# Leaving padded list rows out of gathers and scatters, and starting the second mixture stage inside the last tile of the first

## The reference, cut to what matters

```python
def _L1_ffn_ref(x, P_w, U1, U2, U3, W1, W2, b2):
    # x_flat: 2048 x 256; W1: 12 x 1024 x 256; W2: 12 x 256 x 1024
    x_addr = x_flat @ P_w.T
    dw1 = _route_dense(x_addr @ U1.T, 3, 1.0)   # three of 12 experts per token, softmax of their scores
    dw2 = _route_dense(x_addr @ U2.T, 3, 1.0)
    dw3 = _route_dense(x_addr @ U3.T, 3, 1.0)
    h = sum over e of (x_flat @ W1[e].T * dw1[:, e:e+1])
    h = gelu(h, approximate=False)
    y = sum over e of (h @ W2[e].T * dw2[:, e:e+1])
    return y + dw3 @ b2
x = x + _L1_ffn_ref(_layernorm(x), ...)
```

## Time and profile before

| | before |
|---|---|
| median of three runs | 1073.56 us |
| profiled execution | 1068.93 us |
| its span | 1067.1 us |
| TensorE busy in the span | 1019.5 us (96%) |
| VectorE, ScalarE, GpSimd busy | 618.1, 438.9, 285.0 us |
| first stage on TensorE (L2331) | from 587.8 to 799.2 us |
| second stage on TensorE (L2382) | from 802.8 to 1048.9 us |

### The profile page before, as it was taken

One profiled execution on the slowest core, in us unless ns is written; L12 is line 12 of the kernel. 1 busy time (PEld: TensorE's weight loads), 2 busy tenths in 40 slices (PEclk: granted clock), 3 DMA queues, 4 the chain that ended last, 5 costly groups with the idle time before them and its releaser, 6 DMA issues. The chain is left out here.

```text
span 1067.1 us, 19880 instructions
## 1 busy us (share of the span) xinstructions
PE 1019.5 (96%) x6532; PEld 743.3 (70%) x6532; DVE 618.1 (58%) x1388; ACT 438.9 (41%) x856; POOL 285.0 (27%) x313
## 2 busy tenths in 40 slices
PE   8999999999899999999987999999999999999996
PEld 5888844688899888688875444443347777777784
DVE  6988757776544454565777888676411365323513
ACT  2666644422211223366654355554442233333330
POOL 1221100000011100201102222265623577644441
PEclk9999999999999999999999999999999999999998
DMA  8000050000599100470001544489999999764644
GB/s 238 2 0 0 1 195 0 1 1 1 175 343 351 44 1 0 171 316 1 12 31 33 188 168 173 171 290 380 354 352 410 408 340 344 251 224 147 223 133 173
DMA packets 79950, 177.25 MB, mean 166 GB/s; under 512 B 11581, under 2 KB 32047, under 8 KB 78332
## 3 DMA queue, kind: packets, MB, share of 16 engines
q1 hardware_dynamic: 55250, 102.09, 26.4%
q0 software_dynamic: 20896, 69.75, 19.1%
q10 hardware_dynamic: 3722, 4.33, 1.2%
HBM read 126.06 MB, written 47.97 MB: 163 GB/s over the span
## 5 line engine op out<-in xcount | busy, mean ns | idle before, releaser
L2684 DVE COPY shared<-f_psT 128x256 f32<-128x256 f32 x54 | 22.6, 421 | 145.8 <-PE f_psT L2382 145.8
L2432 ACT ACTIVATE shared<-f_psH 128x512 f32<-128x512 f32 x108 | 64.3, 597 | 103.0 <-PE f_psH L2331 82.5
L2331 PE MATMUL f_psH<-W,ctxT 128*128 (+2 forms) x216 | 99.4, 603 | 4.7 <-ACT f_stage L2453 2.3
L2382 PE MATMUL f_psT<-W,sel 128*64 (+2 forms) x432 | 98.6, 381 | 2.6 <-ACT sel L2461 1.4
L2382 PE MATMUL f_psT<-W,f_xg 128*128 x432 | 97.7, 379 | 0.0
L2331 PE MATMUL f_psH<-W,f_xTk 128*128 (+2 forms) x216 | 97.5, 594 | 0.2 <-ACT shared L2432 0.2
L2382 PEld LDWEIGHTS f_psT<-W,f_xg 128*128 128x128 f32 x432 | 80.1, 190 | 9.8
L2382 PEld LDWEIGHTS f_psT<-W,sel 128*64 128x64 f32 (+2 forms) x432 | 62.0, 148 | 28.5 <-issue 5.9
L2141 POOL DMA_INDIRECT f_xg<-xn_d,f_toks x54 | 53.9, 999 | 102.2 <-PE f_psT L2307 90.0
L2141 POOL DMA_INDIRECT f_temps<-h_d,f_toks x54 | 52.7, 977 | 96.9 <-PE f_psH L2359 77.2
L1581 POOL DMA_DIRECT2D m_eos<-m_eo x32 | 16.8, 525 | 200.5 <-DVE m_eo L1478 199.2
(11 more groups left out here) (357 smaller groups left out, 2188.9 us busy)
## 6 DMA issues: line engine op xcount, KB each, us to landing
p_d<-shared SPq DMA_DIRECT2D x108, 256.0 KB, 2.6
W<-in_f_W1T SPq DMA_DIRECT2D x12, 1024.0 KB, 16.0
W<-in_f_W2T SPq DMA_DIRECT2D x12, 1024.0 KB, 10.6
m_wg<-in_m_Wg SPq DMA_DIRECT2D x16, 512.0 KB, 4.4
m_wu<-in_m_Wu SPq DMA_DIRECT2D x16, 512.0 KB, 5.9
m_wd<-in_m_Wd SPq DMA_DIRECT2D x16, 512.0 KB, 6.2
h_d<-a_W SPq DMA_DIRECT2D x16, 512.0 KB, 6.0
f_g<-p_d SPq DMA_DIRECT2D x8, 384.0 KB, 5.3
```

What stands on the lines that cost most here:

```text
L2331: mm = pe.matmul(psH[at, n % 2, c, :], xTk[n % 2][:, k, at], weights, start=k == 0, stop=k == KD - 1)
L2382: mm = pe.matmul(psT[at, n % 2, 0:D], hT[n % 2][:, k, at], weights, start=k == 0, stop=k == KH - 1)
L2432: act.activation(po[:, n % 2, c * HH:(c + 1) * HH], psH[:, n % 2, c, :], ACT.Copy).then_inc(po_ready, 1)
L2684: dve.tensor_copy(y_out[:, n % OUTS, :], psT[:, n % 2, 0:D]).then_inc(yo_ready, 1)
```

## The change

It has two parts.

**Bounds.** The token table now holds token - 1024 (never 0 in a real row), and 1024 is added to the sums: a real row gives its token, a padded one 1024, which lies outside the 1024 rows of the source. The gathers of tokens and sums (`fetch_held`, new) and the scatter carry a bound, and rows past it are left out: buffers keep what they had there. `xg` and `temps` are therefore set to zero once on GpSimd, before their first gather. The spare rows, their table, its load, and two VectorE operations for each list of the second routing go away. The product gathers (`three`) have no padding and stay.

**Border.** TensorE turns tile 0 of the second stage between the two halves of the last `expand`, and tile 1 in the middle of `contract(0)`. ScalarE passes tile 0 through the gelu ahead of `products(53)`, and asks for the gelu once on one element after tile 50, which brings the table in early. `evicted` waits for each quarter of `po` when it needs it, at tiles 0, 2, 4 and 6. SyncE waits for experts 0 and 1 ahead of the last store and counts them there, then loads 2 and 3, and goes on as before with two loads ahead.

```diff
-    p2_rows = [nc.dram_tensor(f"p2_d{b}", (N * TOP + TB * P, D), F32, kind="Internal").ap() for b in range(B)]
+    p2_rows = [nc.dram_tensor(f"p2_d{b}", (N * TOP, D), F32, kind="Internal").ap() for b in range(B)]
...
-                    one.step(dve.tensor_scalar(pair[:, :], found[:, 0:TB], -1.0, 0.0, ALU.add, ALU.max))
+                    one.step(dve.tensor_scalar(pair[:, :], found[:, 0:TB], float(N), None, ALU.add))
...
-                        one.step(dve.scalar_tensor_tensor(own[:, 0:TB], found[:, 0:TB], 0.0, spare[:, :],
-                                                          ALU.is_equal, ALU.mult))
...
-                        one.step(dve.tensor_tensor(pair[:, :], pair[:, :], own[:, 0:TB], ALU.add))
...
+                    def fetch_held(pool, place, source, index, done):
+
+                        pool.indirect_dma_start(place, None, source, bass.IndirectOffsetOnAxis(ap=index, axis=0),
+                                                bounds_check=N - 1, oob_is_err=False).then_inc(done, 16)
...
-                        pool.wait_ge(list_ready, 1)
                         for i in range(2):
                             pool.wait_ge(xn0_stored[i], 16 * (NT // 2))
+                        pool.memset(xg[:, :, :], 0.0).then_inc(rows_clear, 1)
+                        pool.wait_ge(list_ready, 1)
+                        pool.wait_ge(rows_clear, 1)
...
-                                                        y_out[:, n % OUTS, :], None).then_inc(yo_stored[n % OUTS], 16)
+                                                        y_out[:, n % OUTS, :], None, bounds_check=N * TOP - 1,
+                                                        oob_is_err=False).then_inc(yo_stored[n % OUTS], 16)
...
                             pool.wait_ge(list_ready, 4)
                             pool.wait_ge(dwT_mm, 1)
+                            pool.memset(temps[:, :], 0.0).then_inc(rows_clear, 1)
+                            pool.wait_ge(rows_clear, 2)
                             all_sums(0)
...
                                 for c in range(2):
+                                    if n == LT - 1 and c == 1:
+                                        turn_hidden(0)
...
                                     s = k * D // BANK
+                                    if n == 0 and k == KQ:
+                                        turn_hidden(1)
...
-                            turn_hidden(0)
                             for n in range(LT):
-                                if n + 1 < LT:
+                                if 0 < n < LT - 1:
                                     turn_hidden(n + 1)
                                 contract(n)
...
+                                if n == LT - 1:
+                                    hidden_T(0)
                                 products(n)
+                                if n == LT - 4:
+                                    act.activation(mhalf[0:1, 0:1], ones[:, 0:1], ACT.Gelu)
...
                                 dve.wait_ge(y_mm, 2 * n + 2)
-                                if n == 0:
-                                    for s in range(2):
-                                        for c in range(2):
-                                            dve.wait_ge(po_stored[s][c], landed(LT, s, 2))
+                                if n < OUTS and n * D % HH == 0:
+                                    s, c = divmod(n * D // HH, 2)
+                                    dve.wait_ge(po_stored[s][c], landed(LT, s, 2))
...
+                                if n == LT - 1:
+                                    for e in range(2):
+                                        sp.wait_ge(w2_landed[e % 4], 16 * (e // 4 + 1))
+                                        sp.sem_inc(w2_ld, 1)
                                 store(n)
...
-                            for e in range(2, E1 + 2):
-                                if e < E1:
-                                    load_w2(e)
-                                sp.wait_ge(w2_landed[(e - 2) % 4], 16 * ((e - 2) // 4 + 1))
+                            for e in range(2, 4):
+                                load_w2(e)
+                            for e in range(2, E1):
+                                if e + 2 < E1:
+                                    load_w2(e + 2)
+                                sp.wait_ge(w2_landed[e % 4], 16 * (e // 4 + 1))
                                 sp.sem_inc(w2_ld, 1)
...
-        "c_tokid": flip(np.arange(1, 1 + N, dtype=np.float32).reshape(NT, P)),
-        "c_spare": np.arange(N * TOP, N * TOP + TB * P, dtype=np.float32).reshape(TB, P).T.copy(),
+        "c_tokid": flip(np.arange(-N, 0, dtype=np.float32).reshape(NT, P)),
```

More of the change, by code:

```diff
@@ L141, in build @@
     h_d = [a.rearrange("(i p) h -> i p h", p=P) for a in h_rows]
-    p2_rows = [nc.dram_tensor(f"p2_d{b}", (N * TOP + TB * P, D), F32, kind="Internal").ap() for b in range(B)]
-    p2_d = [a[0:N * TOP, :].rearrange("(i p k) d -> i p k d", k=TOP, p=P) for a in p2_rows]
+    p2_rows = [nc.dram_tensor(f"p2_d{b}", (N * TOP, D), F32, kind="Internal").ap() for b in range(B)]
+    p2_d = [a.rearrange("(i p k) d -> i p k d", k=TOP, p=P) for a in p2_rows]
     out_tiles = out.rearrange("b (t p) d -> (b t) p d", p=P)
@@ L1623, in top3_mixture @@
                 tokid = sb(st, "f_tokid", [P, NT])
-                spare = sb(st, "f_spare", [P, TB])
                 pair = sb(st, "f_pair", [P, TB])
@@ L1915, in loads @@
                         sp.dma_start(tokid[:, :], t["c_tokid"]).then_inc(ld, 16)
-                        sp.dma_start(spare[:, :], t["c_spare"]).then_inc(ld, 16)
                     shifts, shifted = shift, shift_step
@@ L1924, in gpsimd @@
                         pool.memset(ones_b[:, :], 1.0).then_inc(consts, 1)
-                        pool.wait_ge(ld, 16 * 4)
+                        pool.wait_ge(ld, 16 * 3)
                         pool.tensor_copy(below_b[:, :], below).then_inc(consts, 1)
@@ L1999, in vector @@
                         if u == self.CENTRE + 2:
-                            dve.wait_ge(ld, 16 * 4)
+                            dve.wait_ge(ld, 16 * 3)
                             one.step(dve.tensor_tensor(
@@ L2076, in top3_mixture @@
                     owner_ready = sem("f_owner_ready")
+                    rows_clear = sem("f_rows_clear")
                     gap_ready = sem("f_gap_ready")
@@ L2146, in tokens @@
                         wait(pool, xgT_mm, n - QUAD + 1)
-                        fetch(pool, xg[:, n % QUAD, :], xn_d[b], toks[:, 0, b * TB + i:b * TB + i + 1], xg_ld[n % QUAD])
+                        fetch_held(pool, xg[:, n % QUAD, :], xn_d[b], toks[:, 0, b * TB + i:b * TB + i + 1], xg_ld[n % QUAD])
                     def route_sync(sp):
@@ L2259, in hidden @@
                                 wait(pool, hT_mm, 2 * (n - SEATS) + 2)
-                                fetch(pool, hg[:, n % SEATS, :], h_rows[b], toks[:, 1, b * TB + i:b * TB + i + 1], hg_ld[n % SEATS])
+                                fetch_held(pool, hg[:, n % SEATS, :], h_rows[b], toks[:, 1, b * TB + i:b * TB + i + 1],
+                                           hg_ld[n % SEATS])
                             def scatter(n):
@@ L2485, in _ @@
                             act.wait_ge(owner_ready, 2 * B)
-                            hidden_T(0)
                             for n in range(LT):
```

## The result

Seven executions of the changed kernel gave a median of 1080.78 us (1074.78 to 1081.42), seven of the kernel before 1071.9 (1067.73 to 1074.41). The ratio is 1.0068, interval [1.0038, 1.0099]: slower by 0.7%. The median lies outside my range of 1062 to 1078 and on the other side of the forecast of 1.3 us less. All ratios and intervals here are worked out from the single executions, without the few slow ones, and are not the quotients of the medians (1.0083 for this pair). Two later comparisons of the same two kernels gave 1.0023 [0.9983, 1.0062] and 1.0041 [1.0015, 1.0068]. The change costs some 0.2 to 0.7%, 3 to 7 us; the first figure is the highest of the three, and the interval of the second takes in no change at all.

What follows compares the result with a forecast made beforehand. TensorE, busy 1019.5 of 1067.1 us, was taken as the bound, so only its idle time could go. Border -1.7 plus 0.4 given back made -1.3, from 1071.2 to 1069.9 us; range 1062 to 1078.

Steps and rivals of the forecast that it cites:

- forecast of 1.3 us less: Whole kernel: 1.7 us gained at the border, 0.4 given back later; chance 0.40.
- The border: Between the two stages: both turns stay, TensorE's waiting for copy, table and gelu goes; gain 1.7 us.
- The table load: ScalarE's gelu table load of 1.28 us moves behind tile 50, near 789 us, delaying a copy half a microsecond at most.
- Given back: Second stage, gather of tile 10: lands later beside W2 loads, wait of up to 0.9 us, taken as 0.4.
- rival (a): Border gain given back at gathers of tiles 9 and 10: -0.8 us or nothing; 0.10 shared with a do-nothing rival.
- What a bound costs on GpSimd: 846 to 906 us, 24 indirect DMAs with a bound: taken as 0, at worst 10.9 us.
- My threshold for a slower kernel: 846 to 906 us: slower from 0.28 us on each of 24 bounded DMAs, 5.4 us after the forecast gain.
- Rival (b): 846 to 906 us: the bound lengthens each checked GpSimd DMA; at 0.45 us each +9.6 us, 1080.8; chance 0.20.
- Padding: "I take nothing": Padded rows no longer moved, 4.7 of 177 MB: taken as no gain, bounds 1 us lost to 5.3 gained.
- Rival (c): First stage: DMA stalls at 746 and 778 us vanish too, 5.3 us more, -6.6 in all, 1064.6; chance 0.30.
- SyncE, "nothing on the path": Store of tile 53 and W2 loads move later; last load 2.4 us later, VectorE 0.6 us late, TensorE unaffected.
- Fills and VectorE's steps: GpSimd fills of 0.96 and 3.6 us lie in idles; VectorE's two dropped operations per list lie under TensorE's work: nothing.

Runs made afterwards that it cites:

- g4: Kernel before, no bound, with a short fill and wait ahead of each gather of sums and each scatter; ratio 1.0039 [1.0007, 1.0071].
- e4: Kernel before with a bound on the same three kinds of DMA, all indices inside it, nothing left out; ratio 1.0047 [1.0011, 1.0083].
- the second group: Changed kernel again and with 1 MB store held back; before with delayed first gather, and with bounds on sums and scatter; ratios 1.0023, 0.9989, 1.0067, 1.0004.
- e2: Kernel before with the border part alone, SyncE's new order included, no bounds or fills; ratio 1.0008 [0.9974, 1.0042].
- h2: Kernel before with only SyncE's new order, both W2 counts ahead of the store of tile 53; ratio 1.0038 [1.0004, 1.0073].
- g1: Kernel before with the border part alone, but SyncE's old order of the W2 counts; ratio 0.9983 [0.9947, 1.0018].

## Why the prediction was wrong

**The border: right, and given back.** Gain predicted 1.7 us, measured 1.88 (11.24 to 9.36). In other executions it is worth more, for a reason that I had overlooked. In the kernel before, ScalarE's last copy waits not for the product but for an earlier store of products to land; the table load and the gelu come behind it. Here is that copy, and then TensorE in g4, which has the same order at the border:

```profile
800.00 0.60 ACT L2432 ACTIVATE shared<-f_psH 128x512 f32<-128x512 f32 x1 [0.82 <-DMA p_d<-shared]
```

```profile
801.57 0.66 PE L2369 MATMUL f_psH<-ident,f_temps 128*128 128x128 f32 x4 [1.15 <-ACT shared L2442]
803.67 5.40 PE L2392 MATMUL f_psT<-W,sel 128*128 x16 [1.45 <-ACT sel L2471]
```

In g4 TensorE waits for that copy too, ahead of the second turn, and contract(0) then runs in part at 1.2 GHz (5.40 us instead of 3.72). With before's border the stretch is 11.24 us in before and e4, and 11.53 to 15.56 in the six others; with the border part it is 9.36 to 9.40 in all ten.

The table load came at 794.62, 6.5 us ahead of the last product (6.8 predicted). No drain stands between the load and the copy ahead of it, and the small gelu follows within 0.02 us. The Trainium skill's page "ScalarE: Activation LUTs", section "What ACT_TABLE_LOAD costs", has a drain of 1380 ns there; this trace doesn't agree, nor does TensorE wait in the tiles behind it.

**Given back: rival (a), with too small a number.** I took 0.4 us, and at the gather of tile 10. The rows misled me: the landing of 17.3 us in the earlier trace rows is that of a product gather begun at 823.7, not of tile 9's gather of sums, which landed 18.9 us after its start (843.84 - 824.93); and landings count from the start of a DMA, so tile 10's gather was there 3.0 us ahead of its use and not 2.0. Leaving the second group out, as in all means here, the stretch from tile 2 to 13 is 56.2 us in the mean of the eight kernels with the border part, and 53.9 in the five with before's border and SyncE's old order: 2.3 us. The border itself differs by 3.1 us between the same kernels (12.5 and 9.4), so most of the gain is given back, and all of what I had predicted. The two terms that I missed: the wait of tile 9 grows (1.5 to 2.4 us, against 0 to 0.9); and an idle of this length can cost as much again in clock, as e2 shows. The issue of this gather moves with TensorE, as I said against rival (a), but its landing hardly does: it takes 18.9 to 19.8 us from its start with the border part and 15.4 to 18.9 without, and counted from the start of the last product it is there after 46.7 to 47.6 us instead of 47.3 to 48.7.

**"What a bound costs on GpSimd ... I take 0": the step that failed.** It was wrong in kind and in size. In kind, since I looked for the cost in the DMA's length and in one stretch. Its first part is ahead of the DMA: a MOVE and a delay, hidden where GpSimd is busy with the DMA before (the gap stays 0.30 us), visible where it waits. There it is 0.6 us at the first gather and 0.5 at the last scatter, and what follows both is on the path. I had counted the fill of `xg` at this place and nothing else, and the first gather's neighbour, the 1 MB store that started 0.65 us behind the second gather, stood in no row of mine. What followed was 3.6 to 3.8 us, six times the delay; the lower clock behind the wait is part of it. Its second part is the length: over tiles 9 to 27 the median of a gather of sums goes from 962 to 1012 ns, that of a scatter from 996 to 1025. My threshold for a slower kernel was 0.28 us each, at one for one. The runs show 1.7 us (mean 65.8 us of eight kernels with these bounds, 64.1 of five without) for about 34 DMAs x 0.04 = 1.4 us. Rival (b) had this place right, but by its own terms it needed 0.28 us for each DMA to make the kernel slower. The larger loss, at the start, stood in no rival, so it is mostly luck that the kernel came out slower, as (b) said.

**Padding: "I take nothing", worth 3 us.** Over kernels with and without padding, first stage and border differ by 3.3 us without the border part (208.0 against 211.3) and by 2.6 with it (206.3 against 208.9, the latter of two kernels 2.7 us apart). Of the stalls at 746 and 778 us the first is down to 0.25 us in the changed kernel, the second to 1.17. Rival (c) with its 5.3 us was nearer than I. I had it as a way to a faster kernel; it did occur, and other terms covered it.

**SyncE, "nothing on the path": not shown.** The store of tile 53 came at 810.13, 9.0 us behind the start of the last product (805.5 - 795.8 = 9.7 predicted), but the last count later than I had it, at 854.0, where 845.8 + 5.3 = 851.1 was predicted. VectorE's copies of tile 10 waited for it until 854.1, and TensorE did not wait for them. Whether the move costs anything is open: h2's ratio says so, and its trace doesn't.

**Fills and VectorE's steps: right.** 0.95 and 3.53 us (0.96 and 3.6 predicted), both in idles.

**The sum**, from the means: start +3.7, first stage and border together -5.0 (211.3 to 206.3: padding and border part), given back +2.3, GpSimd's stretch +1.7, tail +0.8 (18.5 to 19.3, same groups of kernels; my sum had no term for it), together +3.5 us or 0.3%, within the intervals of the two repeats and 0.1% below the mean of the three ratios (1.0044). At that mean the time would be 1071.9 x 1.0044 = 1076.6, inside the range; the sign of the forecast is wrong either way, and the rest of the first result, 4 us, no part of the traces explains. A slip of the prediction that changes nothing: its idle times and the clock add up to 8.8 us and not 8.9.

## What to carry to other kernels

An option on an instruction can cost ahead of it and not in it: ask at which of its sites the engine comes out of a wait, because here only there did the delay show. Look at what starts within a microsecond of each moved transfer on other queues; here a short transfer that slipped behind a large one lost several times the slip, and TensorE's clock added to it. Time won just ahead of a wait on a transfer is mostly not won, unless the transfer itself moves. And when a time to landing is read from a view, check which DMA it belongs to.

## What the hardware showed that I had not expected

- A bound brings a MOVE of 0.03 us, and with it the indirect DMA starts 0.5 to 0.6 us later where GpSimd had been waiting (eleven traces each at the first gather and at the last scatter), and by nothing that shows where it had not (0.30 us between two DMAs with and without).
- A gather of 128 rows of 1 KB issued together with a 1 MB store was usable after 5.4 us (6.2 when the store was 0.15 us ahead), against 3.2 when it was 0.65 us ahead of the store and 2.9 without it. The Trainium skill's page "DMA: Bandwidth & Descriptors", section "SWDGE vs HWDGE vs iDMA", lets the two kinds of queue take turns on an engine; the two extra microseconds agree with that.
- Idles of 1.8 to 3.4 us of TensorE were followed by 1.2 GHz in some places (4 us at 594, part of 8 us at 840 in e2) and not in others (1.89 us in g1, whose next tiles ran at 1.00). What decides it these runs don't show.
